# Small inputs in one transfer, the decays' squares on GpSimd, and another order for the first y's two parts

## What is computed

```
def mix(r, k, v, w, u, time_emb):              # used twice, k = v = f
    tf = sigmoid(sum(time_emb))
    decay = exp(-exp(w)) * (0.5 + 0.5 * tf)
    a, b = scans forward and backward over positions of exp(k)*v and exp(k), each with `decay`
    num = a_fwd + a_bwd - exp(k)*v + exp(min(u + k, 30)) * v
    den = b_fwd + b_bwd - exp(k)   + exp(min(u + k, 30))
    return sigmoid(r) * num / max(den, 1e-8) * (0.8 + 0.2 * tf)
x = x + attention(mix(x, f, f, w1, u1, cond_512))          # 16 heads of 128, causal
x = x + experts(mix(x, f, f, w2, u2, cond_512))            # best 2 of 8, softmaxed
```

## Time and profile before

| | |
|---|---|
| three executions | 369.21, 369.50, 369.51 us; median 369.5 us |
| the profiled execution | 369.06 us, its span 367.2 us (1.9 us lie around it) |
| PE busy | 343.4 us (94% of the span) |
| PE weight loads busy | 317.8 us (87%) |
| DVE busy | 316.0 us (86%) |
| ACT busy | 255.8 us (70%) |
| POOL busy | 217.3 us (59%) |
| DMA | 14.13 MB, mean 38 GB/s |

### The profile page before, as it was taken

The page is one execution under the profiler, slowest core; times in us unless marked ns, Lnnn a source line. Parts: engine busy times, 40 slices in busy tenths (PEclk is TensorE's granted clock), DMA queues, the critical chain, the costliest instruction groups (busy, mean ns, idle before and its releaser), DMA issues.

```text
span 367.2 us, 7428 instructions
## 1 busy us (share of the span) xinstructions
PE 343.4 (94%) x2404; PEld 317.8 (87%) x2404; DVE 316.0 (86%) x889; ACT 255.8 (70%) x685; POOL 217.3 (59%) x227
## 2 busy tenths in 40 slices
PE   0896699999999999999999999999999989899997
PEld 0685589998999999999999999999999979788885
DVE  4978999999899989999999999998768576869675
ACT  5869898788878969896988888788778565321100
POOL 4876778854746578966877876697564424310000
PEclk9999999999999999999999999999999999999999
DMA  4560026100000000130100031100000000000000
GB/s 153 197 221 4 0 82 208 43 20 0 2 0 3 1 2 2 47 127 1 52 7 3 1 112 64 58 2 2 1 3 0 2 1 2 0 16 14 29 29 30
DMA packets 4613, 14.13 MB, mean 38 GB/s; under 512 B 848, under 2 KB 1888, under 8 KB 3936
## 3 DMA queue, kind: packets, MB, share of 16 engines
q1 hardware_dynamic: 4352, 13.66, 11.0%
q10 hardware_dynamic: 224, 0.01, 0.0%
HBM read 12.60 MB, written 1.05 MB: 37 GB/s over the span
## 4 chain that ended last, share of the span: by engine, by line
PE 75%; DVE 14%; ACT 4%; DMA 2%; issue 2%; POOL 2%; DVEq 0%; ACTq 0%; POOLq 0%
PE psQK L962 8%; PE psQK L960 8%; PE psQK L961 8%; PE psT L1030 5%; PE psO L960 4%; PE psO L962 4%; PE psO L961 4%; PE psV L960 4%; PE psS L960 3%; PE psZ L1043 3%; PE psS L1016 3%; PE psS L962 3%; PE psS L961 3%; PE psV L962 3%; PE psV L961 3%
## 5 line engine op out<-in xcount | busy, mean ns | idle before, releaser
L326 POOL TENSOR_SCALAR prob<-prob,rsum 128x256 f32<-128x256 f32 x60 | 56.3, 939 | 56.9 <-DVE rsum L778 56.6
L536 ACT ACTIVATE prob<-prob,ntop 128x256 f32<-128x256 f32 (+1 forms) x128 | 57.1, 449 | 24.9 <-DVE ntop L770 24.5
L960 PE MATMUL psQK<-y_hi,w_hi 128*128 128x256 f32 x256 | 72.4, 283 | 1.9 <-DVE y_lo L702 1.5
L962 PE MATMUL psQK<-y_hi,w_lo 128*128 128x256 f32 x256 | 72.4, 283 | 0.0
L961 PE MATMUL psQK<-y_lo,w_hi 128*128 128x256 f32 x256 | 72.3, 282 | 0.0
L332 POOL TENSOR_TENSOR z_lo<-z_lo,z_two 128x256 fp32r<-128x256 f32 x64 | 48.3, 755 | 34.9 <-DVE z_lo L796 34.9
L291 POOL TENSOR_TENSOR w_lo<-raw,w_hi 128x512 fp32r<-128x512 f32 x40 | 54.3, 1368 | 2.8 <-ACT w_hi L396 2.7
L960 PEld LDWEIGHTS psQK<-y_hi,w_hi 128*128 128x128 f32 x256 | 48.7, 190 | 3.9 <-POOL w_lo L291 2.7
L782 DVE TENSOR_TENSOR qk<-psQK,qk 128x512 fp32r<-128x512 f32 x64 | 43.3, 677 | 8.1 <-ACT qk L524 8.1
L961 PEld LDWEIGHTS psQK<-y_lo,w_hi 128*128 128x128 f32 x256 | 48.7, 190 | 1.2
L962 PEld LDWEIGHTS psQK<-y_hi,w_lo 128*128 128x128 f32 x256 | 48.8, 191 | 0.0
(11 more groups left out here) (163 smaller groups left out, 1034.9 us busy)
## 6 DMA issues: line engine op xcount, KB each, us to landing
raw<-in_weights SPq DMA_DIRECT2D x5, 1024.0 KB, 6.5
raw<-in_weights SPq DMA_DIRECT2D x10, 512.0 KB, 4.5
out<-fT SPq DMA_DIRECT2D x8, 128.0 KB, 1.7
fT<-in_fT SPq DMA_DIRECT2D x2, 256.0 KB, 5.5
xT<-in_xT SPq DMA_DIRECT2D x2, 256.0 KB, 6.6
fT<-in_fT SPq DMA_DIRECT2D x1, 512.0 KB, 5.4
xT<-in_xT SPq DMA_DIRECT2D x1, 512.0 KB, 6.7
temb<-in_temb ACTq DMA_DIRECT2D x1, 1.0 KB, 3.4
```

The costliest lines, as they stand in the source:

```text
L326: pool.tensor_scalar(prob[:, k, P:3 * P], prob[:, k, P:3 * P], rsum[:, k, 1:2], None, ALU.mult).then_inc(shared, 1)
L536: ins = act.activation(prob[:, k, lo:hi], prob[:, k, lo:hi], ACT.Exp, scale=-1.0, bias=ntop[:, k, q:q + 1], accum_out=ssum[:, k, q:q + 1])
L960: pe.matmul(out, ah, bh, start=first and k == 0, stop=False)
L962: ins = pe.matmul(out, al, bh, start=False, stop=last and k == n - 1)
```

## The change

Four edits:

1. `temb` and `wu` become one tensor `small`, 128 x 12, loaded by one DMA on ACT's queue. Numbers and readers are the same.
2. `rest` is made on GpSimd for both layers, as `(1 - decay)` times `(decay + 1)`: three instructions on 128 x 8 in place of DVE's two, with a new tile `decay_one` and a new semaphore `rested` which ACT's scaling waits for. For layer 1 they stand ahead of GpSimd's clamp L364; for layer 2 in unit 10 after the table's pieces and ahead of that unit's scaling L326. DVE's `decays(1)` goes from unit 10 to unit 8.
3. ACT's `y_hi` of half 0 goes ahead of condition 1's exponentials.
4. Reciprocal 1 is made in two instructions of 128 columns, with y_lo 0 between them. The counts waited for follow (y_lo 1 is now 21).

The tables are written out in full in another form, with the same places. Apart from the rows below, every engine has the same instructions in the same order.

```diff
-        act.dma_start(temb[:], ap["temb"]).then_inc(in_temb, 16)
-        act.dma_start(wu[:], ap["wu"]).then_inc(in_wu, 16)
-        act.wait_ge(in_wu, 16)
+        act.dma_start(small[:], ap["small"]).then_inc(in_small, 16)
+        act.wait_ge(in_small, 16)
...
+        def rests(w):
+            pool.wait_ge(pre_dve, 3 + 2 * w)
+            pool.tensor_scalar(rest[:, w], decay[:, w], -1.0, 1.0, ALU.mult, ALU.add).then_inc(rested, 1)
+            pool.tensor_scalar(decay_one[:, w], decay[:, w], 1.0, None, ALU.add).then_inc(rested, 1)
+            pool.wait_ge(rested, 2 + 3 * w)
+            pool.tensor_tensor(rest[:, w], rest[:, w], decay_one[:, w], ALU.mult).then_inc(rested, 1)
+
+        at(10, "M", rests, 1)
+
+
+        rests(0)
         pool.wait_ge(f_act, 3)
...
-        act.wait_ge(pre_dve, 5)
+        act.wait_ge(rested, 3)
...
+        first_y_high(0)
         cond(1)["exps"]()
-        first_y_high(0)
         first_y_high(1)
...
         dve.wait_ge(pre_dve, 3)
-        rests(0)
         dve.wait_ge(f_act, 1)
...
-        at(10, "M", late_rests)
...
+        at(8, "M", decays, 1)
...
         first_product(0)
-        first_reciprocal(1)
+        first_reciprocal(1, slice(0, P))
         first_y_low(0)
+        first_reciprocal(1, slice(P, T))
         first_product(1)
         first_y_low(1)
```

More of the change, by code:

```diff
@@ L58 @@
[L58 to L62, removed]
[3 rows of a table removed]
-FIRST_O = (4, 5)
+COND_DVE_AT = {
[7 rows of a table added]
+}
+COND_ACT_AT = {
[7 rows of a table added]
+}
+COND_POOL_AT = {
[7 rows of a table added]
+}
+REFILL_ACT = (
+    ("qk", 1, 0, -1, "E"),
+    ("qk", 1, 1, 0, "E"),
+    ("v", 1, 0, 1, "E"),
+    ("qk", 1, 2, 2, "E"),
+    ("v", 1, 1, 2, "E"),
+    ("qk", 1, 3, 3, "E"),
+    ("o", 1, 0, 8, "E"),
+    ("o", 1, 1, 9, "E"),
+    ("qk", 2, 0, 25, "E"),
+    ("qk", 2, 1, 26, "E"),
+    ("v", 2, 0, 26, "E"),
+    ("qk", 2, 2, 27, "E"),
+    ("v", 2, 1, 27, "E"),
+    ("qk", 2, 3, 29, "E"),
+    ("o", 2, 0, 33, "E"),
+    ("o", 2, 1, 34, "E"),
+    ("qk", 3, 0, 34, "E"),
+    ("qk", 3, 1, 35, "E"),
+    ("qk", 3, 2, 37, "E"),
+    ("qk", 3, 3, 40, "E"),
+    ("v", 3, 0, 41, "E"),
+    ("v", 3, 1, 42, "E"),
+    ("o", 3, 0, 43, "E"),
+    ("o", 3, 1, 45, "E"),
+    ("v", 4, 0, 48, "E"),
+    ("v", 4, 1, 49, "E"),
+    ("qk", 4, 0, 50, "E"),
+    ("qk", 4, 1, 51, "E"),
+    ("qk", 4, 2, 52, "E"),
+    ("qk", 4, 3, 53, "E"),
+    ("o", 4, 0, 54, "E"),
+    ("o", 4, 1, 55, "E"),
+)
@@ new lines @@
+REFILL_POOL = (
+    ("o", 0, 0, 4, "M"),
+    ("o", 0, 1, 5, "M"),
+    ("qk", 1, 0, 0, "M"),
+    ("qk", 1, 1, 1, "M"),
+    ("v", 1, 0, 2, "M"),
+    ("qk", 1, 2, 3, "M"),
+    ("v", 1, 1, 3, "M"),
+    ("qk", 1, 3, 4, "M"),
+    ("o", 1, 0, 9, "M"),
+    ("o", 1, 1, 10, "M"),
+    ("qk", 2, 0, 26, "M"),
+    ("qk", 2, 1, 27, "M"),
+    ("v", 2, 0, 27, "M"),
+    ("qk", 2, 2, 28, "M"),
+    ("v", 2, 1, 28, "M"),
+    ("qk", 2, 3, 30, "M"),
+    ("o", 2, 0, 34, "M"),
+    ("o", 2, 1, 35, "M"),
+    ("qk", 3, 0, 35, "M"),
+    ("qk", 3, 1, 36, "M"),
+    ("qk", 3, 2, 38, "M"),
+    ("qk", 3, 3, 41, "M"),
+    ("v", 3, 0, 42, "M"),
+    ("v", 3, 1, 43, "M"),
+    ("o", 3, 0, 44, "M"),
+    ("o", 3, 1, 46, "M"),
+    ("v", 4, 0, 49, "M"),
+    ("v", 4, 1, 50, "M"),
+    ("qk", 4, 0, 51, "M"),
+    ("qk", 4, 1, 52, "M"),
+    ("qk", 4, 2, 53, "M"),
+    ("qk", 4, 3, 54, "M"),
+    ("o", 4, 0, 55, "M"),
+    ("o", 4, 1, 56, "M"),
+)
@@ L344, in _, with at, do @@
         work = {}
-        def at(u, f, *args):
-            work.setdefault(u, []).append((f, args))
+        def at(u, place, f, *args):
+            work.setdefault((u, place), []).append((f, args))
         for n in range(1, len(CONDS)):
             pieces = products(n)
[L351 to L360, removed]
+            for name, u, place in COND_POOL_AT[n]:
+                at(u, place, pieces[name])
+        for kind, g, part, u, place in REFILL_POOL:
+            at(u, place, refill, kind, g, part)
+        at(59, "M", y2_low, 0)
+        at(63, "M", y2_low, 1)
+        def do(u, place):
+            for f, args in work.get((u, place), ()):
+                f(*args)
+        def rests(w):
[6 more added lines that the diff above has]
+        rests(0)
         pool.wait_ge(f_act, 3)
@@ L378, in _ @@
                 z_last(u - 4)
-            for f, args in work.get(u, ()):
-                f(*args)
+            do(u, "M")
             if u not in SHARES_ACT:
                 shares(u)
+            do(u, "E")
         for u in range(UNITS - 4, UNITS):
@@ L566, in _ @@
             pieces = cond(n)
[L567 to L572, removed]
+            for name, u, place in COND_ACT_AT[n]:
+                at(u, place, pieces[name])
+        for kind, g, part, u, place in REFILL_ACT:
+            at(u, place, refill, kind, g, part)
         at(10, "E", bias_high_part)
@@ L910, in _ @@
             reciprocals(u)
+            do(u, "V")
             i, h = u // GH, u % GH
@@ L1130, in _ @@
         pe.wait_ge(ones_set, 1)
-        pe.wait_ge(in_temb, 16)
-        pe.matmul(ts, ones[:], temb[:], start=True, stop=True).then_inc(tsummed, 1)
+        pe.wait_ge(in_small, 16)
+        pe.matmul(ts, ones[:], temb, start=True, stop=True).then_inc(tsummed, 1)
         pe.wait_ge(consts, 2 + E)
@@ L1217, in lay_out @@
     wu = np.stack([inputs[n].reshape(CB, P).T for n in ("L0_cond_w", "L0_cond_u", "L0_cond2_w", "L0_cond2_u")], 1)
+    small = np.zeros((P, 4 * CB + B), np.float32)
+    small[:, 0:4 * CB] = wu.reshape(P, 4 * CB)
+    small[0:TD, 4 * CB:] = inputs["cond_512"].T
     return {
@@ L1220, in lay_out @@
         "fT": channels_first(inputs["fside_BxSxS_0"]),
-        "temb": np.ascontiguousarray(inputs["cond_512"].T),
-        "wu": np.ascontiguousarray(wu),
+        "small": small,
         "weights": weights,
```

42 lines of the change are left out of this document (16 added, 26 removed), and 24 rows, old and new, of tables (COND_ACT_AT, COND_DVE_AT, COND_POOL_AT, REFILL).

## The result

| | before | after |
|---|---|---|
| median of 8 runs each | 369.40 us | 368.19 us |
| lowest to highest | 369.12 to 369.51 | 368.02 to 368.52 |
| profiled execution, its span | 369.06, 367.2 | 368.02, 366.1 |

Between the two profiled executions the difference is 1.04, where the sum said 1.02.

What follows compares the result with a forecast made beforehand. TensorE was taken to bound from 87 us on, with DVE's time counting before that. Gains of 0.24 and 0.78 sum to 1.02: 369.06 to 368.04 profiled, median 368.5, range 367.7 to 369.4 us (8 in 10).

Steps and rivals of the forecast that it cites:

- the sum: Whole kernel: 0.24 us gained at the start plus 0.78 in units 8 to 13, 1.02 in all.
- The line through two sizes: GpSimd's small instructions: 1.49 us at 512 columns and 0.92 at 256 give 0.35 each, 1.05 for three.
- What the load decides: Unit 0: the second q and k weights' load gates the exponentials (22.93); TensorE's path, maxima ready at 22.56, is second.
- goes on at 17.95: 0.45 earlier: First projections, edits 3 and 4: TensorE starts near 15.9, waits some 0.6 between halves, then continues 0.45 us earlier.
- forecast 0.78: Units 8 to 13: the late sum, DVE at most 0.78 us earlier at unit 13's maxima; ends 0.2 and 1.0.
- more than 0.14: Unit 8: cost of the two decays, 0.36 us less 0.22 in DVE's pause, so 0.14; otherwise 0.46.
- 0.30 to 0.35: Around 73.85 us: z's last step of unit 7 on GpSimd ends at 73.55, so TensorE is 0.3 to 0.35 earlier.
- The port rule: Unit 8: DVE and GpSimd share an SBUF port; the decays are slow only beside a busy GpSimd, cost 0.14.
- A: Rival: the late gain from units 8 to 13 doesn't arrive, 368.9 to 369.4 us; chance 0.22.
- D: Rival: nothing gained at the start, the load 0.15 later, 0.1 + 0.6 in all, 368.8 us; chance 0.10.
- B: Rival: GpSimd's three small instructions take 2.8 us, past the start's cover of 2.1; 370 to 371 us; chance 0.10.
- C: Rival: more than forecast, load 0.3 earlier and late part 0.9 to 1.0; 367.5 to 368.0 us; chance 0.18.

Runs made afterwards that it cites:

- e8: The changed kernel with nine more small GpSimd instructions between GpSimd's three on `rest` at the start; 368.37 us.
- e9: The changed kernel with nine more small GpSimd instructions between GpSimd's three on `rest` in unit 10; 368.62 us.
- e12: The changed kernel with GpSimd's subtraction of the first second-layer q and k weights waiting for the end of DVE's first scan of condition 1; 368.10 us.
- e13: The changed kernel with e12's wait, a like wait ahead of GpSimd's next subtraction, and `decays(1)` moved from unit 8 to unit 2; 367.77 us.
- e7: The changed kernel with ACT's copy of the first second-layer q and k weights moved from ahead of unit 0's exponentials to unit 0's end; 368.17 us.
- e1: The kernel before with only layer 2's `rest` on GpSimd in unit 10 and `decays(1)` in unit 8; 368.60 us, ratio 0.9980.
- e6: The changed kernel with `decays(1)` moved from unit 8 to ahead of DVE's first low part of qk; 368.75 us.
- e11: The changed kernel with two small DVE instructions ahead of the scans of condition 1, which hold them back; 368.49 us.
- e5: The changed kernel without edits 3 and 4; 368.32 us.
- e4: The kernel before with only edit 1, the one load; 369.35 us, ratio 0.9999.
- e2: The kernel before with only layer 1's `rest` on GpSimd; 369.21 us, ratio 0.9995.
- e3: The kernel before with only edits 3 and 4; 369.20 us, ratio 0.9998.

## Why the prediction was right

**Edit 1**: 0 forecast, 0.36 possible. `small` landed after 3.28, between the two rows that served as bounds; 0.09 of gain in the trace. Alone it gives 369.35 against 369.36.

**Edit 2 at the start**: the mechanism holds: first scan at 5.49 where it said 5.55, the load issued at 16.91 where it said 16.93, exponentials at 22.63 where it said 22.69. That they fit so closely is partly luck, since 0.09 of them is edit 1's, which was put at 0; edit 2's own part is 0.21, not 0.24. GpSimd's three took 0.69, not 1.05. The line through two sizes overstated them: at 8 columns one takes 0.20 to 0.24, and 0.16 in a row of like ones. The 1.0 us that the prediction worked out beside it counted two inputs for each of the three; only the last has two, and it took 0.20, no more than the first. Its verdict stood because it was compared with a cover, which e8 measured at 2.14.

**What the load decides**: this step is half right. "What decides when unit 0's softmax goes on is the load" is true in the two profiled executions and in those of e9, e12 and e13, and e7, which takes this gate away, has unit 0's exponentials at 22.19. It isn't in the executions in which GpSimd's subtraction comes ahead of DVE's second scan (e1 to e6, e8, e11): there DVE's queue from the maxima on is the path. The prediction took the median's 0.44 above the profiled execution as a constant. I read it as this: the profiled execution of before had DVE first (scans 1.27 us), and most others, by their times, had not. After's runs lie from 368.02 to 368.52, the profiled one lowest, so its median is only 0.17 above. That missing 0.27 is nearly all of the 0.3 between forecast and result, and not a gain of any edit that the sum had priced. Some 0.10 of it is that the median of three executions was 369.50 and that of eight is 369.40; the rest is inferred from the times, since one execution of each kernel has a trace. Whether the early edits made the good order more frequent is open. In the two traces they moved both sides alike, the end of the maxima by 0.31 and the start of the subtraction by 0.30, and no run forces the order in the kernel before.

**Edits 3 and 4**: worth 0, as forecast; but the step "goes on at 17.95: 0.45 earlier" was loose. It measured against a TensorE that had not been moved, though 0.30 of it is the start's. The cut also cost more than 0.1: the second y_lo is 0.09 earlier than in the earlier trace rows where the start alone would give 0.30, so 0.21. Both ways end the same eighteen matmuls at 19.04, as e5's chain shows. The remark that they would decide if the load came 0.6 earlier falls too: e11's path does come through y, and even there both ways, with the edits (e11) and without (e5), end at 19.04.

**Edit 2 in units 8 and 10**: forecast 0.78, e1 alone 0.76, lead in the traces 0.24 to 1.03. The decays' pair took 0.33 in unit 8 (forecast 0.36, the rival's bound 0.68), but cost more than 0.14: 0.25 by e13, 0.27 by e6. The term was mis-sized by what comes behind. DVE itself was on time again at the next maxima (62.67; 62.66 in e13), but the unit's reciprocals had been only 0.03 earlier than in before, so GpSimd's scaling and its next instructions started late, and DVE's product at 63.89 took 1.43 beside them where e13 shows 1.17. With that the early lead was nearly gone on DVE and GpSimd when unit 10 began (0.03 at 67 to 68 us). There the four instructions gave the whole 1.00: the reciprocals start 1.03 earlier. z's last step gained 0.73 rather than 0.30 to 0.35, since GpSimd's three took 0.69 and not 1.05. There is a slip in the working too: that 0.30 to 0.35, and the 0.78 made from it, count from the times of before and so already hold what is left of the early lead, yet the sum adds 0.24 to them. By the same step the measured 0.73 and the 0.43 of unit 13 give 1.16 for the whole lead, and the trace shows 1.13. So a cost and a gain that were both set too low and a lead counted twice cancel; that 1.02 meets 1.04 so closely is luck, while the mechanism, DVE's microsecond reaching TensorE by 86 us, is shown by e1.

The port rule that the prediction weighed was borne out for the decays: 0.33 us with GpSimd at rest, 0.83 near the end of its instruction, 2.48 behind two. What the prediction missed is that the same effect sat on the path at 22 us, where it changed the time by as much as the early edits. There the Trainium skill (SBUF — State Buffer, SBUF: two separate sides) says more than what the prediction cited from it: the shared pair is an exclusive lock, also against a DVE instruction with two SBUF inputs, and whoever starts first has it for the whole instruction. The scans read `decay` and a tile in SBUF, and e11 and e12 agree with it: 2.32 against 1.27. That the second of the two ends a fixed time after the first, 0.55 or 1.09, agrees with it too; e9 shows that the recorded starts don't name the first when they are 0.04 us apart.

**Rivals.** A and D didn't come. B's cover was right at the start and its place right in unit 10, at a quarter of its price per instruction. C's time was near, for another reason than it gave.

## What to carry to other kernels

When the runs of a kernel spread by more than their noise, ask which of them the profile is: two orders of the same instructions, decided by 0.1 us of a transfer's landing, can differ in what the critical path even is. A wait can fix the good order: e12 lies 0.39 us below e11 in the median, though only 0.09 below after, whose profiled execution has that order by itself. Ahead of moving a small instruction into an engine's pause, look at what GpSimd does there, not at whether the engine is idle. Price a small step against its cover, and measure the cover by padding it.

## What the hardware showed

- DVE and GpSimd hold each other up by order of start: the scan pair takes 1.27 us when its second scan is first and 2.28 to 2.38 when GpSimd's 1.30 us subtraction is; in the first case the subtraction takes 1.53 to 1.79 instead. Whichever is second ends a fixed time after the first: the scan 0.54 to 0.55 us after the subtraction (eight traces), the subtraction 1.09 to 1.10 after the scan (five traces). A pair of 4-column instructions took 2.48 behind two GpSimd instructions.
- An instruction of 8 columns on GpSimd takes 0.20 to 0.24 us, 0.16 each in a row of nine.
- TensorE's granted clock fell to 0.50 at 31 to 33 us in seven of the fourteen profiled executions, behind the wait for v's low part: after waits of 2.16 us (e11), 2.05 (e1), 2.02 (e4 and e8), 2.01 (e2), 1.96 (e6) and 1.83 (e7), but not after 2.06 (e3), 2.02 (e5) or 1.68 (after). So the length of this one wait doesn't tell which. Windows of e11 (columns as for the stages):

```profile
30.00:31.80 1.80, 1.05 (x3) 0.89 (x4) 1.35 (x7) 1.77 (x5) 1.80 (x2) 0.66 0.03 9
31.80:33.00 1.20, 1.20 (x4) 0.93 (x3) 0.44 (x1) 1.20 (x5) 0.92 (x2) 0.50 0.00 0
```

Half of full clock is the level of 1.2 GHz; matmuls of 512 columns were then 0.43 apart instead of 0.23. It cost nothing that lasts: TensorE's lag in e11 behind after was 0.47 ahead of the dip, 1.52 in it, 0.65 at 33.45, where both wait for pT, and 0.49 at 40 us.
